# The base product of three of four token groups written as seven block products, with its weight sums in a scratch and a quarter of the low parts on GpSimd

## Chip, cores and metric

The kernel runs on one core of a Trainium2 chip (trn2). The metric is the device time of one execution in microseconds. The engines are TensorE (PE; its weight loads are PEld), VectorE (DVE), ScalarE (ACT), GpSimd (POOL) and SyncE (SP), which only issues transfers here.

## What is computed

A gated block on 2 x 1024 tokens of 2048 features: first an attention-like product of quantized numbers, then a dense layer with a routed low-rank adapter.

```python
x = x + tanh(g_xattn) * matmul(fake_quant(layernorm(x)), fake_quant(ctx_4096))
h = layernorm(x)
base = einsum('bsd,od->bso', h, base_W)                   # 2048 x 2048 x 2048, float32
probs = softmax(einsum('bsd,ed->bse', h, router_W))       # 8 experts
w_dense = top-2 of probs, scaled to sum 1, else 0
mid = einsum('bsd,edr->bser', h, lora_A) * w_dense[..., None]   # rank 16
x = x + tanh(g_ffn) * (base + 2.0 * einsum('bser,erd->bsd', mid, lora_B))
```

## The kernel before

**First stage (0 to about 305 us).** The 16 token tiles of 128 rows are normalised and quantized, `ctx` is quantized to bf16 (ScalarE, then `ctx_widen` on GpSimd), and TensorE computes 64 units (a token tile by 512 columns, 16 matmuls each) in the order of a table, `UNITS`. VectorE takes each unit out of PSUM (`evac`), and GpSimd adds a column term (`add_col_term`). When all tiles of a token group have a block, ScalarE's queue stores it to a scratch in HBM, `x1s` (`store_x1`). Tables of slots (`UNIT_SLOT`, `COLADD_SLOT` and others) set the order in which each engine takes its work; every engine walks the same slots and works in the order in which it finds its own. Its time is set by waits on semaphores, not by the slot number.

**Second stage.** Four groups `g` of 512 tokens (`M` = 4 tiles) follow. Rows of a group come back from `x1s` (`load_group`), VectorE takes their statistics and normalises them, TensorE transposes them (`transpose_h`), and ScalarE and VectorE split each transposed slice in two float32r parts, `hT_hi` and `hT_lo` (`h_hi`, `h_lo`). The weights come in pieces of 128x1024 (`WK` = 2 slices of the 2048 inputs by `NW` = 512 outputs) through a ring of four: ScalarE copies the high part (`w_hi`), VectorE subtracts to get the low part (`w_lo`). A float32 product is three matmuls (`three`): high by high, high by low, low by high. A group runs over `NB` = 4 blocks of 512 outputs; a piece feeds 2 slices x 4 tiles x 3 = 24 matmuls. At the end of a block the adapter's product (three matmuls a tile) is added in the same bank, VectorE adds the residual (L823), and the rows are stored. Behind a group the next one's router and adapter input are computed (`ar_slice`, 128 matmuls of 272 columns). Groups 0 to 2 are a loop on every engine (`Fori`), the last is written out.

## Time and profile before

| | |
|---|---|
| Times of 3 runs | 1162.58, 1166.63 (median), 1169.81 us |
| Profiled execution | 1168.86 us, of which span 1167.1 us |
| Mean granted clock of TensorE | 0.982 of full speed |
| Busy: TensorE, its weight loads, VectorE, ScalarE, GpSimd | 94%, 70%, 47%, 26%, 16% |
| Moved by DMA | 195.98 MB, 168 GB/s over the span |

The span runs from the first instruction to the last. The shares are means over both stages; GpSimd works in the first one only.

### The profile page before, as it was taken

How to read it: one execution, taken by the hardware profiler on the slowest of the kernel's cores; microseconds unless marked ns; L12 is line 12 of the kernel's file. 1: busy time of each engine (PE TensorE's matmuls, PEld its weight loads, DVE VectorE, ACT ScalarE, POOL GpSimd, SP SyncE). 2: the span in 40 equal slices, each digit the busy share in tenths (PEclk: the TensorE clock that was granted, in tenths of full speed). 3: DMA queues.
4: the chain of work that ended last, by engine and by line, in shares of the span. 5: the costliest groups of instructions: out<-in, count | busy, mean ns of one | idle time of the engine just before them, and what ended most of it. 6: DMA issues, size and time to landing. Idle time of an engine off the chain costs nothing.

```text
span 1167.1 us, 13452 instructions
## 1 busy us (share of the span) xinstructions
PE 1092.7 (94%) x5136; PEld 817.9 (70%) x5136; DVE 547.9 (47%) x832; ACT 301.5 (26%) x299; POOL 185.8 (16%) x123
## 2 busy tenths in 40 slices
PE   0679996999899999998999999989999999999998
PEld 0234442444698888887888887878888889888887
DVE  7696567955763542443238234333633343222231
ACT  5554244600232212221212213211212331111210
POOL 3584768743200000000000000000000000000000
PEclk9999998999899999998999999989999999999999
DMA  8897797757662533507242623441533504152440
GB/s 332 297 340 238 278 292 252 240 144 255 217 251 75 199 95 140 183 34 289 72 143 74 217 88 128 136 194 58 191 115 102 198 34 147 54 203 83 147 145 37
DMA packets 90699, 195.98 MB, mean 168 GB/s; under 512 B 38928, under 2 KB 40976, under 8 KB 82448
## 3 DMA queue, kind: packets, MB, share of 16 engines
q1 hardware_dynamic: 39696, 153.18, 35.6%
q10 hardware_dynamic: 50944, 41.95, 12.6%
q8 instruction: 45, 0.74, 0.3%
q14 instruction: 14, 0.11, 0.0%
HBM read 153.16 MB, written 33.55 MB: 160 GB/s over the span
## 4 chain that ended last, share of the span: by engine, by line
PE 84%; issue 3%; DVE 3%; ACT 3%; DMA 2%; POOL 2%; ACTq 2%; SPq 0%; DVEq 0%; POOLq 0%
PE acc L877 18%; PE acc L879 18%; PE acc L878 18%; PE acc L855 14%; PE acc_even L877 3%; PE acc_even L878 3%; PE acc_even L879 3%; ACTq L503 2%; PE aT_psum L892 1%; PE aT_psum L914 1%; PE aT_psum L915 1%; ACT ctx_u L490 1%; POOL ctx_quant L435 1%; DMA w_stage<-in_wt 1%; PE acc L914 1%
## 5 line engine op out<-in xcount | busy, mean ns | idle before, releaser
L877 PE MATMUL acc<-w_hi,hT_hi 128*128 128x512 f32 x896 | 354.2, 395 | 0.0
L879 PE MATMUL acc<-w_hi,hT_lo 128*128 128x512 f32 x896 | 350.6, 391 | 0.0
L878 PE MATMUL acc<-w_lo,hT_hi 128*128 128x512 f32 x896 | 350.3, 391 | 0.0
L732 DVE TENSOR_TENSOR w_lo<-w_stage,w_hi 128x1024 fp32r<-128x1024 f32 x128 | 156.7, 1224 | 320.8 <-ACT w_hi L544 319.3
L544 ACT ACTIVATE w_hi<-w_stage 128x1024 fp32r<-128x1024 f32 x128 | 135.6, 1059 | 460.1 <-PE acc L879 324.3
L879 PEld LDWEIGHTS acc<-w_hi,hT_lo 128*128 128x128 f32 x896 | 169.0, 189 | 36.2
L878 PEld LDWEIGHTS acc<-w_lo,hT_hi 128*128 128x128 f32 x896 | 169.3, 189 | 34.0
L877 PEld LDWEIGHTS acc<-w_hi,hT_hi 128*128 128x128 f32 x896 | 169.2, 189 | 34.0
L855 PE MATMUL acc<-ctx_quant,aT_even 128*128 128x512 bf16 x512 | 117.0, 388 | 43.5 <-POOL ctx_quant L435 41.1
L855 PEld LDWEIGHTS acc<-ctx_quant,aT_even 128*128 128x128 bf16 x512 | 50.4, 100 | 108.7 <-issue 44.7
L855 PE MATMUL acc<-ctx_quant,aT_odd 128*128 128x512 bf16 x512 | 115.6, 388 | 7.8 <-POOL ctx_quant L435 5.8
L855 PEld LDWEIGHTS acc<-ctx_quant,aT_odd 128*128 128x128 bf16 x512 | 50.8, 100 | 71.7 <-issue 14.2
L490 ACT ACTIVATE ctx_u<-ctx_stage,scalars,constants 128x2048 uint8<-128x2048 f32 x32 | 66.4, 2087 | 72.5 <-issue 50.5
L823 DVE SCALAR_TENSOR_TENSOR residual<-acc,gates,residual 128x512 f32<-128x512 f32 x56 | 42.0, 750 | 69.7 <-PE acc L879 69.7
L435 POOL TENSOR_SCALAR ctx_quant<-ctx_u 128x2048 bf16<-128x2048 uint8 x32 | 64.3, 2011 | 51.0 <-ACT ctx_u L490 44.7
L743 DVE TENSOR_TENSOR hT_lo<-aT_psum,hT_hi 128x512 fp32r<-128x512 f32 x48 | 32.6, 690 | 67.6 <-ACT hT_hi L552 67.6
L877 PE MATMUL acc_even<-w_hi,hT_hi 128*128 128x512 f32 x128 | 51.2, 400 | 7.7 <-issue 7.7
L552 ACT ACTIVATE hT_hi<-aT_psum 128x512 fp32r<-128x512 f32 x48 | 28.0, 597 | 96.5 <-PE aT_psum L892 96.5
L878 PE MATMUL acc_even<-w_lo,hT_hi 128*128 128x512 f32 x128 | 50.4, 394 | 0.0
L879 PE MATMUL acc_even<-w_hi,hT_lo 128*128 128x512 f32 x128 | 50.3, 393 | 0.0
L449 POOL TENSOR_TENSOR x_group_odd<-x_group_odd,col_term 128x512 f32<-128x512 f32 x32 | 43.3, 1358 | 36.0 <-DVE x_group_odd L671 36.0
L449 POOL TENSOR_TENSOR x_group_even<-x_group_even,col_term 128x512 f32<-128x512 f32 x32 | 42.2, 1333 | 20.8 <-DVE x_group_even L671 10.7
(126 smaller groups left out, 977.0 us busy)
## 6 DMA issues: line engine op xcount, KB each, us to landing
w_stage<-in_wt SPq DMA_DIRECT2D x128, 512.0 KB, 5.9
ctx_stage<-in_ctx SPq DMA_DIRECT2D x32, 1024.0 KB, 7.7
x_group_even<-x_scratch SPq DMA_DIRECT2D x16, 1024.0 KB, 10.0
residual<-x_scratch SPq DMA_DIRECT2D x64, 256.0 KB, 3.9
out<-residual ACTq DMA_DIRECT2D x64, 256.0 KB, 2.8
x_group_even<-in_x SPq DMA_DIRECT2D x8, 1024.0 KB, 7.1
x_group_odd<-in_x SPq DMA_DIRECT2D x8, 1024.0 KB, 9.7
x_scratch<-x_group_even ACTq DMA_DIRECT2D x8, 1024.0 KB, 5.6
```

What stands on the lines that cost most here:

```text
L435: pool.tensor_scalar(ctxq[:, c % NB, PK * p:PK * (p + 1), :], cu8[q % 2][:, :, :], -MID, 1.0, ALU.add, ALU.mult).then_inc(c_conv, 1)
L449: pool.tensor_tensor(blk, blk, colb[n][:, :], ALU.add).then_inc(x1_ready, 1)
L490: act.activation(cu8[q % 2][:, :, :], cst[q % CS][:, :, :], ACT.Identity, scale=inv2, bias=z2).then_inc(cu8_ready, 1)
L544: act.activation(wh[s][:, :], wst[s][:, :], ACT.Copy).then_inc(wh_ready, 1)
L552: act.activation(hh[:, k, :], h_psum(g, k), ACT.Copy).then_inc(hh_ready, 1)
L732: dve.tensor_tensor(wl[s][:, :], wst[s][:, :], wh[s][:, :].bitcast(F32), ALU.subtract)\
L743: dve.tensor_tensor(hl[:, k, :], h_psum(g, k), hh[:, k, :].bitcast(F32), ALU.subtract)\
L823: dve.scalar_tensor_tensor(out=res[m][:, :], in0=bank(j, m)[:, :], scalar=gate2, in1=res[m][:, :], op0=ALU.mult, op1=ALU.add)\
L855: ins = pe.matmul(acc[p % M][:, :], aT[g % 2][:, k, m * P:(m + 1) * P], ctxq[:, c % NB, k, :], start=(k == 0), stop=(k == K - 1))
L877: pe.matmul(out_, lh, rh, start=first, stop=False)
L878: pe.matmul(out_, lh, rl, start=False, stop=False)
L879: return pe.matmul(out_, ll, rh, start=False, stop=final)
```

## The change

Group 0 keeps its product. In groups 1 to 3 the 512 x 2048 x 2048 product is cut in two halves of outputs, and each half (512 tokens x 2048 inputs x 1024 outputs) in two by two blocks of each operand: A11, A12, A21, A22 of the tokens, transposed (256 tokens by 1024 inputs each), and B11 to B22 of the weights. It is then computed as seven block products instead of eight, in Winograd's form of Strassen's algorithm. With S1 = A21 + A22, S2 = S1 - A11, S3 = A11 - A21, S4 = A12 - S2 and T1 = B12 - B11, T2 = B22 - T1, T3 = B22 - B12, T4 = T2 - B21 (up to signs) the products are those of `COMBO` with `RIGHT`. One product is a *slot*: two token tiles x 8 slices x 3 = 48 matmuls, fed by four pieces of which each serves 12 matmuls. A group has 14 slots; `ROLE` and `FRESH` say in which pair of PSUM banks a slot works and whether it adds to what stands there. Seven times in each half of a group VectorE adds a pair of banks to one of three accumulators (`add_out`), and four of the seven are then stored.

- The weight sums T1 to T4 are computed once, by GpSimd, in eight jobs (`t_job`, four instructions of 128x1024 each), and stored to a scratch in HBM, `w_sums_scratch`. Three jobs stand in the first stage (`JOB_A_SLOT`), five in group 0.
- The token sums S1 to S4 are computed by GpSimd (`combo`) and one difference by VectorE (`diff`), ScalarE and VectorE split all of them in high and low parts (`combo_round`, `combo_rest`). For the next group this stands in slots 11 to 14 and in slot 1.
- All pieces (also the router's, which are loaded again in each group, and the adapter's) go through one list, `PIECES`: a ring of six for the loaded and the low part (`RAW`), a ring of four for the high part (`HI`). High and low parts are made three pieces ahead, loads are asked for five ahead. In groups 1 to 3 GpSimd makes the low part of one piece of each slot (`on_pool`).
- A group's normalised rows are transposed earlier, during slots 5, 6, 7 and 10 (`fill`). Nothing is a loop any more; all groups are written out.

```diff
--- before.py
+++ after.py
-WG = NB * WP
-RING = 4
-LEAD = 2 * RING
-CHAIN_B = 58
+RAW = 6
+HI = 4
...
+SLOTS_G = 14
+JOBS = 8
+JOBS_A = 3
+JOB_A_SLOT = [2120, 2260, 2400]
+RAW_B = ("B11", "B21", "B12", "B22")
+SUM_B = ("T1", "T4", "T3", "T2")
+COMBO = ("A11", "S1", "S2", "S4", "S3", "A12", "A22")
+RIGHT = ("B11", "T1", "T2", "B22", "T3", "B21", "T4")
+ROLE = (0, 1, 0, 1, 0, 1, 0)
+FRESH = (True, True, False, False, False, True, False)
+LORA = (None, None, None, "top_right", "bottom_right", "top_left", "bottom_diff")
+CBUF = (0, 2, 1, 1, 2, 0, 1)
+LOADS_RES = (True, True, True, False, False, False, True)
+STORES = (False, False, False, True, True, True, True)
...
+def on_pool(i):
+    g, kind, s, pc = PIECES[i]
+    return g >= 1 and kind == "W" and pc == 1
...
+    half, r = (s - 1) // 7, (s - 1) % 7
+    return 2 * ((ROLE[r] + half) % 2) + part
...
+            def load_piece(i):
+                g, kind, s, pc = PIECES[i]
+                raw = wst[i % RAW]
+                if i >= RAW:
+                    wait_used(sp, i - RAW)
+            def store_job(j):
+                sp.wait_ge(job_step, 4 * (j + 1))
+                dst = wts[(j // 4) * 2 * WP * P:(j // 4 + 1) * 2 * WP * P, :]
+                sp.dma_start(dst.rearrange("(a q p) n -> q p a n", q=4, p=P)[j % 4], job[j][:, :, :])\
+                    .then_inc(job_stored[j], 16)
...
+            load_job(0)
+            load_job(1)
+            store_job(0)
+            load_job(2)
             sp.wait_ge(x1_stored[0], 16 * NB * 2)
-            load_group(0)
-            sp.wait_ge(pe_unit, max(last_of_tile(t) for t in range(2 * M, 3 * M)) + 1)
-            for r in range(RING):
-                load_lead(r, r)
-            for X in range(RING):
-                sp.wait_ge(wl_ready, X + 1)
-                load_w(X)
+            load_group0()
+            store_job(1)
+            sp.wait_ge(c_conv, 2 * NB * CP)
+            sp.wait_ge(job_stored[1], 16)
+            for i in range(RAW - 1):
+                load_piece(i)
+            store_job(2)
...
+            def t_job(j):
+                pool.wait_ge(job_in[j], 16)
+                b11, b21, b12, b22 = (job[j][:, a, :] for a in range(4))
+                pool.tensor_tensor(b11, b12, b11, ALU.subtract).then_inc(job_step, 1)
+                pool.wait_ge(job_step, 4 * j + 1)
+                pool.tensor_tensor(b12, b22, b12, ALU.subtract).then_inc(job_step, 1)
+                pool.wait_ge(job_step, 4 * j + 2)
+                pool.tensor_tensor(b22, b22, b11, ALU.subtract).then_inc(job_step, 1)
+                pool.wait_ge(job_step, 4 * j + 3)
+                pool.tensor_tensor(b21, b21, b22, ALU.subtract).then_inc(job_step, 1)
             for s in range(SLOTS):
+                if s in JOB_A_SLOT:
+                    t_job(JOB_A_SLOT.index(s))
...
+            def w_lo(i):
+                pool.wait_ge(wh_ready, i + 1)
+                pool.tensor_tensor(wl[i % RAW][:, :], wst[i % RAW][:, :], wh[i % HI][:, :].bitcast(F32),
+                                   ALU.subtract).then_inc(wl_by_pool, 1)
+
+            def combo(dst, a, b, op, h):
+                pool.tensor_tensor(half(dst, h), half(a, h), half(b, h), op).then_inc(combo_sum, 1)
+
+            for i, (g, kind, s, pc) in enumerate(PIECES):
+                if i + HI - 1 < N_PIECES and on_pool(i + HI - 1):
+                    w_lo(i + HI - 1)
...
+                    if s == 12 and pc in (0, 1):
+                        pool.wait_ge(s3_diff, 2 * g + pc + 1)
+                        if pc == 0:
+                            pool.wait_ge(acc_done, done_count(g, 10, 1))
+                        combo(csum["S2"], hf["A22"], hf["A11"], ALU.subtract, pc)
+                    if s == 12 and pc in (2, 3):
+                        if pc == 2:
+                            pool.wait_ge(acc_done, done_count(g, 11, 1))
+                        combo(csum["S4"], hf["A12"], hf["A22"], ALU.subtract, pc - 2)
+                    if s == 13 and pc in (0, 1):
+                        pool.wait_ge(combo_sum, sum_count(g, "S4", pc))
+                        combo(csum["S4"], csum["S4"], hf["A11"], ALU.add, pc)
...
+            def w_hi(i):
+                g, kind, s, pc = PIECES[i]
+                act.wait_ge(w_in[i % RAW], 16 * (i // RAW + 1))
+                if i >= HI:
+                    wait_used(act, i - HI)
...
+                if ends_slot(i - 1):
+                    add_out(*PIECES[i - 1][0:3:2])
+                ahead = i + HI - 1
+                if ahead < N_PIECES:
+                    if not on_pool(ahead):
+                        w_lo(ahead)
...
+                    if s == 11 and pc in (1, 2):
+                        combo_rest(g, "A11", pc - 1)
+                    if s == 11 and pc == 3:
+                        for h in range(2):
+                            diff(g, h)
+                    if s == 12 and pc in (2, 3):
+                        combo_rest(g, "S1", pc - 2)
+                    if s == 13 and pc in (1, 2):
+                        combo_rest(g, "S2", pc - 1)
+                    if s == 13 and pc == 3 or s == 14 and pc == 0:
+                        combo_rest(g, "S3", pc == 0)
+                    if s == 14 and pc in (1, 2):
+                        combo_rest(g, "S4", pc - 1)
+                    if s == 14 and pc == 3:
+                        for h in range(2):
+                            combo_rest(g, "A12", h)
...
+            def slot(g, s):
+                r = (s - 1) % 7
+                name = COMBO[r]
+                high, low = chi[name], clo[name]
+                pe.wait_ge(combo_lo, refill_count(g - 1, name, 1))
+                for pc in range(4):
+                    i = INDEX[g, "W", s, pc]
+                    wait_lo(pe, i)
+
+                    def product(t, kk):
+                        k, part = WK * pc + kk, slice(kk * NW, (kk + 1) * NW)
                         if k == 0:
-                            pe.wait_ge(out_ready, g * ITS + ITS)
-
-            with pe.Fori(0, G - 1) as g:
-                group(g, False)
-            group(G - 1, True)
+                            pe.wait_ge(c_added, bank_free(g, s, t))
+                        last = LORA[r] is None and k == HK - 1
+                        return three(bank(g, s, t)[:, :], high[:, k, tok(t)], low[:, k, tok(t)], wh[i % HI][:, part],
+                                     wl[i % RAW][:, part], FRESH[r] and k == 0, last, not FRESH[r])
...
+            for g in range(1, G):
+                for s in range(1, SLOTS_G + 1):
+                    slot(g, s)
+                    if s == 1:
+                        for k in range(K):
+                            ar_slice(g, k)
```

**The order on GpSimd, end of the first stage.** Before (rows `x_group_...<-..., col_term` are `add_col_term`):

```order
99 L449 TENSOR_TENSOR x_group_even<-x_group_even,col_term_64 128x512
100 L449 TENSOR_TENSOR x_group_odd<-x_group_odd,col_term_65 128x512
101 L449 TENSOR_TENSOR x_group_even<-x_group_even,col_term_67 128x512 x2
102 L449 TENSOR_TENSOR x_group_odd<-x_group_odd,col_term_64 128x512
103 L449 TENSOR_TENSOR x_group_odd<-x_group_odd,col_term_65 128x512 x2
104 L449 TENSOR_TENSOR x_group_odd<-x_group_odd,col_term_66 128x512
105 L449 TENSOR_TENSOR x_group_odd<-x_group_odd,col_term_67 128x512
106 L449 TENSOR_TENSOR x_group_odd<-x_group_odd,col_term_66 128x512 x2
```

and now:

```order
103 L682 TENSOR_TENSOR x_group_even<-x_group_even,col_term_64 128x512
104 L682 TENSOR_TENSOR x_group_odd<-x_group_odd,col_term_65 128x512
105 L682 TENSOR_TENSOR x_group_even<-x_group_even,col_term_67 128x512
106 L687 TENSOR_TENSOR t_job_128<-t_job_128 128x1024
107 L689 TENSOR_TENSOR t_job_128<-t_job_128 128x1024
108 L691 TENSOR_TENSOR t_job_128<-t_job_128 128x1024
109 L693 TENSOR_TENSOR t_job_128<-t_job_128 128x1024
110 L682 TENSOR_TENSOR x_group_even<-x_group_even,col_term_67 128x512
111 L682 TENSOR_TENSOR x_group_odd<-x_group_odd,col_term_64 128x512
112 L682 TENSOR_TENSOR x_group_odd<-x_group_odd,col_term_65 128x512 x2
113 L687 TENSOR_TENSOR t_job_129<-t_job_129 128x1024
114 L689 TENSOR_TENSOR t_job_129<-t_job_129 128x1024
```

Weight-sum jobs stand between the adds: here job 1 (`t_job_128`) ahead of the last add for group 2's tiles, and then job 2.

**The order on VectorE, end of a group.** Before, in the last block of a loop turn (`hT_lo` is the next group's low part, read from PSUM):

```order
458 L823 SCALAR_TENSOR_TENSOR residual_87<-acc,gates,residual_87 128x512
459 L821 REGISTER_ALU
460 L823 SCALAR_TENSOR_TENSOR residual_88<-acc,gates,residual_88 128x512
461 L731 REGISTER_ALU
462 L732 TENSOR_TENSOR w_lo_79<-w_stage_71,w_hi_75 128x1024
463 L742 REGISTER_ALU
464 L743 TENSOR_TENSOR hT_lo<-aT_psum,hT_hi 128x512
465 L742 REGISTER_ALU
466 L743 TENSOR_TENSOR hT_lo<-aT_psum,hT_hi 128x512
467 L731 REGISTER_ALU
468 L732 TENSOR_TENSOR w_lo_76<-w_stage_68,w_hi_72 128x1024
```

and now, slots 11 and 12 of group 1 (`c_acc` rows are `add_out`, `A_lo` and `S_lo` are `combo_rest`, `hT_A_88` is `diff`):

```order
519 L1219 SCALAR_TENSOR_TENSOR c_acc_99<-acc,gates,c_acc_99 128x512 x2
520 L1145 TENSOR_TENSOR w_lo_119<-w_stage_113,w_hi_105 128x1024
521 L1143 TENSOR_TENSOR w_lo_120<-w_stage_114,w_hi_102 128x512
522 L1246 TENSOR_TENSOR A_lo<-hT_A_88,A_hi 128x1024
523 L1145 TENSOR_TENSOR w_lo_121<-w_stage_115,w_hi_103 128x1024
524 L1246 TENSOR_TENSOR A_lo<-hT_A_88,A_hi 128x1024
525 L1237 TENSOR_TENSOR hT_A_88<-hT_A_88,hT_A_90 128x1024 x2
526 L1219 SCALAR_TENSOR_TENSOR c_acc_99<-acc,gates,c_acc_99 128x512 x2
527 L1145 TENSOR_TENSOR w_lo_117<-w_stage_111,w_hi_105 128x1024
528 L1145 TENSOR_TENSOR w_lo_118<-w_stage_112,w_hi_102 128x1024
529 L1143 TENSOR_TENSOR w_lo_119<-w_stage_113,w_hi_103 128x512
530 L1145 TENSOR_TENSOR w_lo_120<-w_stage_114,w_hi_104 128x1024
```

The halves of combinations, of which each reads two tensors in SBUF, stand between the low parts of the pieces.

**The order on GpSimd, the same place.** Before, its queue ended with the first stage's last add. Now, slots 11 to 14 of group 1 (`S_sum` rows are `combo`):

```order
159 L707 TENSOR_TENSOR w_lo_117<-w_stage_111,w_hi_103 128x1024
160 L711 TENSOR_TENSOR S_sum<-hT_A_90,hT_A_91 128x1024 x2
161 L707 TENSOR_TENSOR w_lo_116<-w_stage_110,w_hi_104 128x1024
162 L711 TENSOR_TENSOR S_sum<-hT_A_91,hT_A_88 128x1024 x2
163 L711 TENSOR_TENSOR S_sum<-hT_A_89,hT_A_91 128x1024
164 L707 TENSOR_TENSOR w_lo_121<-w_stage_115,w_hi_105 128x1024
165 L711 TENSOR_TENSOR S_sum<-hT_A_89,hT_A_91 128x1024
166 L711 TENSOR_TENSOR S_sum<-S_sum,hT_A_88 128x1024 x2
167 L707 TENSOR_TENSOR w_lo_120<-w_stage_114,w_hi_102 128x1024
168 L707 TENSOR_TENSOR w_lo_119<-w_stage_113,w_hi_103 128x1024 x2
```

Two, three or one of the sums stand between two low parts that TensorE waits for.

## Rows read from the trace of the kernel before

**Rows 1.** The page: the span, and each engine's busy time (share) and instructions.
```profile
span 1167.1 us, 13452 instructions
...
PE 1092.7 (94%) x5136; PEld 817.9 (70%) x5136; DVE 547.9 (47%) x832; ACT 301.5 (26%) x299; POOL 185.8 (16%) x123
```

**Rows 2.** TensorE's timeline: start, length (us), engine, line, operation, shapes; idle before.
```profile
401.01 0.39 PE L877 MATMUL acc<-w_hi,hT_hi 128*128 128x512 f32 x1
401.24 0.39 PE L878 MATMUL acc<-w_lo,hT_hi 128*128 128x512 f32 x1
...
542.91 0.28 PE L914 MATMUL aT_psum<-ar_hi_lo,hT_hi 128*128 128x272 f32 x1
543.03 0.29 PE L915 MATMUL aT_psum<-ar_hi_lo,hT_lo 128*128 128x272 f32 x1
547.16 0.79 PE L877 MATMUL acc_even<-w_hi,hT_hi 128*128 128x512 f32 x1 [3.84 <-issue]
...
552.34 0.40 PE L877 MATMUL acc_even<-w_hi,hT_hi 128*128 128x512 f32 x1
```

**Rows 3.** Who TensorE waits for, 302 us on: us in total, times, longest.
```profile
PE acc_even L877 <- issue: 7.7, 2, 3.8
PE acc L914 <- DVE ar_hi_lo L724: 2.4, 1, 2.4
```

**Rows 4.** Windows: length; busy PE, PEld, DVE, ACT, POOL; granted clock, DMA share, GB/s.
```profile
543.30:547.00 3.70, 0.02 (x1) 0.00 (x0) 3.36 (x16) 0.23 (x1) 0.00 (x0) 0.78 1.01 421
547.00:551.00 4.00, 3.84 (x9) 3.08 (x10) 3.42 (x15) 0.00 (x0) 0.00 (x0) 0.50 1.00 410
```

**Rows 5.** Groups by line and shape from 333 us on: busy us, mean ns of one.
```profile
L732 DVE TENSOR_TENSOR w_lo<-w_stage,w_hi 128x1024 fp32r<-128x1024 f32 x124 | 151.8, 1224 | 319.8 <-ACT w_hi L544 318.3
...
L823 DVE SCALAR_TENSOR_TENSOR residual<-acc,gates,residual 128x512 f32<-128x512 f32 x56 | 42.0, 750 | 69.7 <-PE acc L879 69.7
...
L738 DVE TENSOR_TENSOR b_lo<-w_stage,b_hi 128x512 fp32r<-128x512 f32 x2 | 1.3, 684 | 0.0
...
L544 ACT ACTIVATE w_hi<-w_stage 128x1024 fp32r<-128x1024 f32 x124 | 131.4, 1060 | 460.1 <-PE acc L879 324.3 <-DMA w_stage<-in_wt 135.8
```

**Rows 6.** GpSimd's timeline in the first stage.
```profile
27.88 1.97 POOL L441 TENSOR_SCALAR x_group_even<-x_group_even,row_terms 128x2048 f32<-128x2048 f32 x1 [0.79 <-DVE row_terms L648]
...
37.32 1.90 POOL L435 TENSOR_SCALAR ctx_quant<-ctx_u 128x2048 bf16<-128x2048 uint8 x1 [2.07 <-ACT ctx_u L490]
39.20 4.00 POOL L441 TENSOR_SCALAR x_group_even<-x_group_even,row_terms 128x2048 f32<-128x2048 f32 x1
...
262.77 1.27 POOL L449 TENSOR_TENSOR x_group_even<-x_group_even,col_term 128x512 f32<-128x512 f32 x1 [2.19 <-DVE x_group_even L671]
```

**Rows 7.** VectorE's timeline beside it.
```profile
37.81 3.55 DVE L656 TENSOR_TENSOR ctx_pair_sums<-ctx_quant 128x4096 f16<-128x4096 bf16 x1
...
108.50 2.28 DVE L656 TENSOR_TENSOR ctx_pair_sums<-ctx_quant 128x4096 f16<-128x4096 bf16 x1
```

**Rows 8.** The end of the first stage on all engines, from their timelines.
```profile
244.47 1.98 POOL L441 TENSOR_SCALAR x_group_odd<-x_group_odd,row_terms 128x2048 f32<-128x2048 f32 x1 [7.17 <-DVE row_terms L648]
...
253.71 10.74 ACTq L510 DMA_DIRECT2D x_scratch<-x_group_even  x2
...
268.25 2.06 SPq L350 DMA_DIRECT2D x_group_even<-x_scratch  x4
...
279.81 2.46 DVE L608 BATCH_NORM_STATS2 bn_chunks_group<-x_group_even 128x6 f32<-128x512 f32 x4
...
305.44 0.66 PE L892 MATMUL acc_even<-identity_f,x_group_even 128*128 128x128 f32 x4 [2.15 <-DVE x_group_even L686]
...
309.70 0.57 PE L914 MATMUL acc<-ar_hi_lo,hT_hi 128*128 128x272 f32 x1 [2.35 <-DVE ar_hi_lo L724]
```

**Rows 9.** DMA issues: how often, KB each, median us from issue to landing.
```profile
w_stage<-in_wt SPq DMA_DIRECT2D x128, 512.0 KB, 5.9
...
x_group_even<-x_scratch SPq DMA_DIRECT2D x16, 1024.0 KB, 10.0
```

More of the change, by code:

```diff
@@ new lines, with pieces @@
+LOADS_RES = (True, True, True, False, False, False, True)
+STORES = (False, False, False, True, True, True, True)
+REFILL = {0: ("S1", "S2", "S3", "A11", "S4", "A21", "A12", "A22"),
+          1: ("A11", "S1", "S2", "S3", "S4", "A12", "A21", "A22")}
+def pieces():
+    order = [(0, "AR", 0, pc) for pc in range(WP)]
+    for n in range(NB):
+        order += [(0, "W", n + 1, pc) for pc in range(WP)] + [(0, "L", n + 1, WP)]
+    for g in range(1, G):
+        for s in range(1, SLOTS_G + 1):
+            order += [(g, "W", s, pc) for pc in range(4)]
+            if LORA[(s - 1) % 7]:
+                order.append((g, "L", s, 4))
+            if s == 1:
+                order += [(g, "AR", 1, pc) for pc in range(WP)]
+    return order
@@ new lines, with lo_count, ends_slot, done_count @@
+PIECES = pieces()
+INDEX = {piece: i for i, piece in enumerate(PIECES)}
+N_PIECES = len(PIECES)
+def on_pool(i):
+    g, kind, s, pc = PIECES[i]
+    return g >= 1 and kind == "W" and pc == 1
+def lo_count(i, pool):
+    return sum(on_pool(e) == pool for e in range(i + 1))
+def ends_slot(i):
+    if i < 0:
+        return False
+    g, kind, s, pc = PIECES[i]
+    return kind == "W" and pc == (WP - 1 if g == 0 else 3)
+def done_count(g, s, part):
+    return M * (s - 1) + part + 1 if g == 0 else M * NB + 2 * SLOTS_G * (g - 1) + 2 * (s - 1) + part + 1
@@ new lines, in closes, with used_count, bank_of, bank_free @@
+def closes(i):
+    g, kind, s, pc = PIECES[i]
+    if kind == "AR":
+        return "ar" if pc == WP - 1 else None
+    if kind == "L" or ends_slot(i) and g >= 1 and not LORA[(s - 1) % 7]:
+        return "slot"
+    return None
+def used_count(i):
+    return sum(closes(e) is None for e in range(i + 1))
+def bank_of(g, s, part):
+    if g == 0:
+        return "even" if part == 0 and s % 2 == 1 else part
+    half, r = (s - 1) // 7, (s - 1) % 7
+    return 2 * ((ROLE[r] + half) % 2) + part
+def bank_free(g, s, part):
+    history = [(0, n + 1, m) for n in range(NB) for m in range(M)]
+    history += [(a, b, t) for a in range(1, G) for b in range(1, SLOTS_G + 1) for t in range(2)]
+    mine = history.index((g, s, part))
+    before = [h for h in history[:mine] if bank_of(*h) == bank_of(g, s, part)]
+    return done_count(*before[-1]) if before else 0
@@ L137, in __call__, with build @@
             self.eng.wait_ge(self.sem, self.base + self.n)
-def build(nc, x, ctx, wt, ar, lb, scal, x1s, out):
+def build(nc, x, ctx, wt, ar, lb, scal, x1s, wts, out):
     es = ExitStack()
@@ L236, in build, with bank @@
         acc0b = psum("acc0_even", [P, NW], F32)
-        def bank(j, m):
-            return acc0b if m == 0 and j % 2 == 0 else acc[m]
-        arp = [acc[0], colp, tpb[0], tpb[1]]
+        def bank(g, s, part):
+            b = bank_of(g, s, part)
+            return acc0b if b == "even" else acc[b]
+        arp = [[acc[0] if g == 0 else acc0b, colp, tpb[0], tpb[1]] for g in range(G)]
         th0 = [acc0b, acc[1], acc[2]]
@@ L415, in _ @@
+            uses = (NB + 2 * (G - 1), NB + 4 * (G - 1), 2 * (G - 1))
+            for b in range(3):
+                sp.wait_ge(out_stored[b], 32 * uses[b])
         @block.gpsimd
@@ L980, in _, with plain_product @@
-            with pe.Fori(0, G - 1) as g:
-                group(g, False)
-            group(G - 1, True)
+                    transpose_h(k + 3)
+            def plain_product(n, pp, m, kk):
+                i = INDEX[0, "W", n + 1, pp]
+                k, part = WK * pp + kk, slice(kk * NW, (kk + 1) * NW)
+                if k == 0:
+                    if bank_free(0, n + 1, m):
+                        pe.wait_ge(c_added, bank_free(0, n + 1, m))
+                    if n == 1 and m == 0:
+                        pe.wait_ge(mid_read, 1)
+                high, low = h_parts(0, k, m)
+                return three(bank(0, n + 1, m)[:, :], high, low, wh[i % HI][:, part], wl[i % RAW][:, part],
+                             k == 0, False)
```

956 lines of the change are left out of this document (664 added, 292 removed).

## The prediction

> **What bounds the kernel now.** The page comes first: TensorE is busy for 94% of the 1167.1 us span, VectorE for 47%, ScalarE for 26%, and GpSimd has done all of its 16% before the first 305 us are over [rows 1]. The busy time of a pipelined TensorE doesn't say that it runs at its pace, so the second view is its own timeline. In the base product a 128x512 matmul starts 0.227 us after the one before (401.01, 401.24), and a router matmul of 272 columns 0.125 us after [rows 2]. The base stage is therefore TensorE's row of matmuls, one behind another: VectorE and ScalarE wait for it, not it for them. The view of waits bears that out: from 302 us on its longest total is 7.7 us, at the two returns of the group loop, where nothing in the profile releases it, and the next is 2.4 us, once, on the way into group 0 [rows 3]. At 543 us TensorE stands for 3.84 us, and the 12 matmuls behind it take 547.16 to 552.34, 5.18 us, where 12 x 0.227 = 2.72 is the pace; the granted clock is 0.50 there, the lower level, 1.2 GHz [rows 2, 4]. Each return thus costs 3.7 + 2.5 = 6.2 us.
>
> **What is removed.** A group had 4 blocks x 16 slices x 4 token tiles x 3 = 768 base matmuls. In groups 1 to 3 it becomes 14 slots x 8 slices x 2 tiles x 3 = 672. The adapter's 48 and the router's 128 stay, and so do the 64 transposes of a group. So 3 x 96 = 288 matmuls go, at 0.227 us each: 65.3 us, all of it on the path. The group loops are written out, so both returns go as well: 2 x 6.2 = 12.4 us. Bounds of that: nothing (a fetch wait stays somewhere) and 12.4; the straight code of the last group has no such wait [rows 3], so I take 12.4. TensorE alone would give 1167.1 - 65.3 - 12.4 = 1089.4 us. The tail is of the same kind as before (one addition, one store).
>
> **What the shorter product asks of the other engines.** A piece of weights (128x1024) used to feed 24 matmuls, 5.44 us; now it feeds 12, 2.72 us, and 56 pieces are prepared in a group, not 32. ScalarE's high part takes 1.06 us and VectorE's low part 1.22 [rows 5], both shorter than 2.72. High and low parts are made three pieces ahead: 8.2 us less 1.1 + 1.2 for the work leaves some 5.8 us by which VectorE may be late before TensorE stands. The part of an adapter piece is wanted already when the slot's last piece begins, so there it is 3 us. On average all fits; what counts is where the new work is bunched.
>
> **The end of a group is such a place.** Slots 11 to 14 hold 4 x 54 = 216 matmuls, 49.0 us. In them VectorE (second fence of the change's order) makes 12 low parts and 14 halves of combinations at 1.22 us, four adapter parts and a difference at 0.68, and 8 additions at 0.75: 31.8 + 3.4 + 6.0 = 41.2 us. GpSimd makes 4 low parts and 8 sums, each 128x1024 with two inputs in SBUF. Its add of 128x512 takes 1.26 to 1.27 us [rows 6], so twice that, 2.5 us: 12 x 2.5 = 30 us. Side by side, both fit into 49.
>
> Do they run side by side? The rows say no. VectorE's pair sum, two inputs in SBUF, takes 2.28 us alone (108.50), but 3.55 at 37.81: GpSimd's instruction of 37.32 ends at 39.2, and 39.2 + 2.3 is its end. GpSimd's row term, 1.97 us alone, takes 4.00 at 39.20, since VectorE's sum runs until 41.4 [rows 6, 7]. Each stood until the other was through. If float32 instructions do the same, VectorE's 35.2 us with two SBUF inputs and GpSimd's 30 have to follow one another: 65 us in 49. The 16 us too many, less the lead of 5.8, leave about 10.5 us that TensorE waits; VectorE's additions read PSUM and don't exclude GpSimd, but hold up its next low part, and an adapter part has the shorter lead. I take 12 us a transition, two of them (from 1 to 2 and from 2 to 3; the last group has no sums): 24 us. Bounds: 0, if the lock doesn't hold here or the next 27 us (slot 1 and the router) take up the rest, and 20 each if additions and waits for each other's results add up. The nearest rows are the two at 37 and 39 us, so I stay near the middle.
>
> The Trainium skill has a rule for it (SBUF — State Buffer, Who interferes with whom): a VectorE instruction with two SBUF inputs contends with a GpSimd instruction that reads SBUF, whoever is first holds the shared pair for its whole length, and the other blocks. It speaks against giving low parts to GpSimd. By that rule the 24 us stand; by each engine's own durations alone they would be 0, and the sum 1105. The trace agrees with the rule at 37.81 and 39.20, for bf16 and for one-input GpSimd work; no row of it has two float32 tensor_tensor beside each other.
>
> **The way into group 1** has the old and the new form together. In the first three pieces of slot 1 VectorE has 4 additions and 8 halves of combinations (S4, A21, A12, A22) besides its low parts, about 12.2 us in two pieces of 2.72, and ScalarE 8 copies at 1.06. The router's third slice pair then comes about 3.5 us late and its first waits about 1: 5 us, bounds 0 and 10. In each of the three groups the adapter's low part stands behind a tile's statistics on VectorE while slot 4's last piece waits for it: 1 us each, 3 in all, bounds 0 and 9.
>
> **The end of the first stage.** GpSimd gets three weight-sum jobs of four 128x1024 instructions, 10 us each, ahead of adds that it made at once. Job 0 can start at 246.4, after the row term of 244.47 [rows 8]. It ends at 256.6, seven adds catch up until 265.4, job 1 ends at 275.5, and the last add of group 2's tiles comes at 276.8; its store was issued at 264 (253.71 + 10.74), and is now near 277. Before, the loads of group 0's rows were issued at 268.25, 4 us behind; now at 281. Their median landing was 10.0 us for four in a row [rows 9]; I put the first at 287, an estimate. So VectorE's statistics start there and not at 279.81 [rows 8]. Since VectorE is nearly always busy from there until TensorE's first transpose at 305.44, that moves by about the same 7 to 8 us; TensorE's units themselves have four banks and go on. The next thing late is the adapter and router weights, whose ring lies where job 2's data were: its store is queued behind four megabytes and ends near 311 (an estimate from 421 GB/s). So the first router slice, at 309.70 before, comes near 318: **+8 us**, bounds 1 (the loads had time to spare) and 18 (jobs also late by their own loads).
>
> **Transfers.** A group of 187 us moves 29 MB of weights, 5 of adapter and router weights, 4 of rows and 8 of residuals and output: 46 MB, 246 GB/s. At 543 us the queues moved 421 GB/s [rows 4], so the rate is there. A piece is asked for five pieces ahead, 13.6 us; less 2.3 for its parts it must land in 11. It took 5.9 us, 10.0 where four loads of a megabyte stood in a row [rows 9]. I take 0. In group 0 the jobs add 20 MB to about 20 over 115 us, 350 GB/s, with a lead of 27 us: 0 too.
>
> **The sum.** 1089.4 + 8 + 5 + 24 + 3 = 1129.4 us of span. The profiled execution has 1.8 us around its span and lies 2.2 us above the median of the three runs (1168.86, 1166.63), so 1131.2 as profiled and **1129** as the median.
>
> **Rivals.**
> - *All hidden.* The lock costs nothing that the lead doesn't cover, since GpSimd's sums are wanted only slots later. Then 1089.4 + 4 + 2 + 2, about 1098 (1088 to 1110). For it: over a whole group VectorE and GpSimd together need less than TensorE. Against: 65 us in 49 at the end of a group.
> - *The lock costs double.* If each low part stands behind one of GpSimd's sums every time, and the lower clock follows the stops as at 547 us, a transition costs 20 to 25 and other slots a few: 1145 to 1165.
> - *The weight ring starves, slower than before.* Its place is the load of a piece in groups 1 to 3. If it lands L us after issue, a piece can't go faster than (L + 2.3) / 5. From L = 11.3 TensorE waits at every piece. With the 8 us of the first stage alone, 1167 is passed when each of the 168 pieces takes 0.42 us more, 3.14, which is L = 13.4. At L = 15 it is 3.46 a piece, 124 us in all, near 1220. For it: 10.0 in [rows 9], where requests queue, and each megabyte of rows goes in front of pieces. Against: the rate shown.
> - *The product is not shorter in effect.* If accumulating over an old result in PSUM made matmuls slower than 0.227, 10% would eat the gain. Every matmul but a bank's first accumulates today at this pace; small.
>
> **How the numbers follow.** 40% for the forecast's own case (1112 to 1145), 28% all hidden, 15% the double price, 10% starved or another stop of every slot (above 1178), 7% something between 1155 and 1178. The range leaves out about 15 to 20%: 1094 to 1160. A measurement can tell about 1% here, 1155 to 1178 being no change: faster 0.82 (the first two and most of the third), same 0.08, slower 0.10.
>
> **What would show it.** Matmul spacing 0.227 us in the slots, and no stop of 3.84 us. GpSimd rows of 2.5 us that lengthen to 3.7 and VectorE rows of 1.22 that lengthen up to 3.7, most of all in slots 11 to 14; there TensorE waits for a low part of VectorE's, 8 to 15 us a transition. The first router slice near 318. Were TensorE's waits to name the DMA of a weight piece, the third rival holds; were there none at all in slots 11 to 14, the first. What would make me wrong above all is the size of the queue at the group's end, which was worked out from a lead and two sums.

## The result, and the profile after

| | before | after |
|---|---|---|
| Median (lowest to highest) | 1166.74 us (1162.58 to 1169.81, 4 runs) | 1133.87 us (1127.80 to 1137.54, 4 runs) |
| Ratio, 95% interval | | 0.9715 [0.9662, 0.9768] |
| Profiled execution: span | 1167.1 us | 1125.8 us |

The profiled execution took 1127.8 us, the fastest of its four; a second series of the same kernel (below) had a median of 1131.27 us. The forecast was 1129, with a span of 1129.4.

The page of the changed kernel, first its busy times (answers to [rows 1]), then the landing of DMAs ([rows 9]):

```profile
span 1125.8 us, 12711 instructions
...
PE 1031.9 (92%) x4827; PEld 765.3 (68%) x4848; DVE 745.4 (66%) x1004; ACT 448.2 (40%) x480; POOL 449.3 (40%) x223
...
w_stage<-in_wt SPq DMA_DIRECT2D x104, 512.0 KB, 4.4
w_stage<-w_sums_scratch SPq DMA_DIRECT2D x96, 512.0 KB, 4.2
```

TensorE has 309 matmul records fewer (288 went; some are missing from a trace). GpSimd's share went from 16% to 40%, and it is no longer done at 305 us. Weight pieces land sooner after they are asked for than before, 4.4 us against 5.9 in the median; some are asked for late (E9, below).

Who TensorE waits for from 300 us on (total, times, longest), the view that answers to [rows 3]:

```profile
PE acc_even L1393 <- DVE x_group_even L1099: 8.1, 1, 8.1
PE acc L1381 <- DVE w_lo L1145: 7.9, 7, 3.4
PE acc L1381 <- DVE w_lo L1143: 6.3, 2, 3.2
PE aT_psum L1451 <- DVE x_rows L1231: 4.7, 3, 3.1
PE acc L1429 <- DVE ar_hi_lo L1140: 3.1, 1, 3.1
PE acc L1381 <- DVE c_acc L1219: 2.3, 1, 2.3
```

The two stops of 3.8 us that nothing released are gone. In their place are stops in which VectorE is late: at the end of the first stage (8.1 and 3.1), for low parts (14.2 in nine waits, of which 11.6 lie in the two transitions and the rest in slot 4), and in group 0 for a normalised row and an addition (`x_rows`, 3.1 of the 4.7, and `c_acc`). No wait of TensorE names the DMA of a weight piece.

The first transition, TensorE's timeline: the wait for the adapter piece's low part, then one piece at the product's pace, then the next stop and what follows it.

```profile
707.80 0.47 PE L1381 MATMUL acc<-w_hi,S_hi 128*128 128x512 f32 x1 [3.17 <-DVE w_lo L1143]
...
709.95 0.39 PE L1381 MATMUL acc<-w_hi,S_hi 128*128 128x512 f32 x1
710.18 0.39 PE L1382 MATMUL acc<-w_lo,S_hi 128*128 128x512 f32 x1
...
721.02 0.80 PE L1381 MATMUL acc<-w_hi,A_hi 128*128 128x512 f32 x1 [3.42 <-DVE w_lo L1145]
...
724.17 0.63 PE L1382 MATMUL acc<-w_lo,A_hi 128*128 128x512 f32 x1
724.60 0.63 PE L1383 MATMUL acc<-w_hi,A_lo 128*128 128x512 f32 x1
```

The spacing is 0.227 us with accumulation over an old result, as in [rows 2]; behind the second stop it is 0.43 until 726.3, and the window of that stretch (busy times as in [rows 4], then granted clock) shows the lower level, 1.2 GHz:

```profile
721.00:726.00 5.00, 4.98 (x12) 3.92 (x13) 5.00 (x5) 1.36 (x2) 0.00 (x0) 0.50 0.29 112
```

VectorE and GpSimd in the same stretch, from their timelines:

```profile
688.04 3.42 DVE L1246 TENSOR_TENSOR A_lo<-hT_A,A_hi 128x1024 fp32r<-128x1024 f32 x1
691.38 1.21 DVE L1145 TENSOR_TENSOR w_lo<-w_stage,w_hi 128x1024 fp32r<-128x1024 f32 x1
...
699.45 5.45 DVE L1145 TENSOR_TENSOR w_lo<-w_stage,w_hi 128x1024 fp32r<-128x1024 f32 x2
704.82 2.83 DVE L1143 TENSOR_TENSOR w_lo<-w_stage,w_hi 128x512 fp32r<-128x512 f32 x1
707.57 3.42 DVE L1145 TENSOR_TENSOR w_lo<-w_stage,w_hi 128x1024 fp32r<-128x1024 f32 x1
```

```profile
684.60 5.78 POOL L711 TENSOR_TENSOR S_sum<-hT_A,hT_A 128x1024 f32<-128x1024 f32 x2 [4.49 <-ACT hT_A L877]
...
697.15 9.95 POOL L711 TENSOR_TENSOR S_sum<-hT_A,hT_A 128x1024 f32<-128x1024 f32 x3 [1.16 <-DVE hT_A L1237]
707.07 2.84 POOL L707 TENSOR_TENSOR w_lo<-w_stage,w_hi 128x1024 fp32r<-128x1024 f32 x1
709.87 3.39 POOL L711 TENSOR_TENSOR S_sum<-hT_A,hT_A 128x1024 f32<-128x1024 f32 x1
```

The low part of 1.21 us at 691.38 runs while GpSimd stands. Beside GpSimd's sums the same instruction takes 2.7, an `A_lo` that begins beside one takes 3.42, which is one of GpSimd's (2.2) and its own (1.2); and GpSimd's take 3.3 instead of 2.4. Both engines read as busy all the time, and a good part of that time is the other's work.

The end of the first stage, GpSimd's jobs among its adds, the store's waiting loads, VectorE's statistics and TensorE ([rows 8] before):

```profile
264.63 2.35 POOL L687 TENSOR_TENSOR t_job<-t_job 128x1024 f32<-128x1024 f32 x1
...
274.22 1.27 POOL L682 TENSOR_TENSOR x_group_even<-x_group_even,col_term 128x512 f32<-128x512 f32 x1
...
279.68 3.26 SPq L518 DMA_DIRECT2D x_group_even<-x_scratch  x4
...
286.88 2.47 DVE L1021 BATCH_NORM_STATS2 bn_chunks_group<-x_group_even 128x6 f32<-128x512 f32 x4 [7.71 <-DMA x_group_even<-x_scratch]
...
310.63 1.12 PE L1393 MATMUL acc_even<-identity_f,x_group_even 128*128 128x128 f32 x4 [8.08 <-DVE x_group_even L1099]
316.54 0.36 PE L1429 MATMUL acc<-ar_hi_lo,hT_hi 128*128 128x272 f32 x1 [3.08 <-DVE ar_hi_lo L1140]
```

And a place that the prediction did not have, in group 0: VectorE beside a weight-sum job, first VectorE, then GpSimd.

```profile
454.93 0.15 DVE L1026 RECIPROCAL rstd<-std 128x1 f32<-128x1 f32 x1
...
455.56 2.06 DVE L1033 TENSOR_TENSOR rstd<-rstd,newton 128x1 f32<-128x1 f32 x1
457.66 3.45 DVE L1231 TENSOR_SCALAR x_rows<-x_rows,mean_var,rstd 128x2048 f32<-128x2048 f32 x1
```

```profile
455.18 2.43 POOL L687 TENSOR_TENSOR t_job<-t_job 128x1024 f32<-128x1024 f32 x1 [19.51 <-DMA t_job<-in_wt]
457.68 2.34 POOL L689 TENSOR_TENSOR t_job<-t_job 128x1024 f32<-128x1024 f32 x1
460.10 3.21 POOL L691 TENSOR_TENSOR t_job<-t_job 128x1024 f32<-128x1024 f32 x1
```

`rstd<-rstd,newton` has one element a partition and takes 0.16 us elsewhere; here it ends when GpSimd's instruction does (457.62 and 457.61). The row normalisation behind it takes 3.45 us instead of 1.35, and TensorE stands 3.12 us for it at 461.16.

**Where the span went**, against the 1089.4 us that TensorE alone would take:

| place | expected | measured |
|---|---|---|
| end of the first stage (first router slice 309.70, now 316.54) | 8 | 6.8 |
| group 0: waits at 390 and 461, 5.4, and 1.3 of lower clock | 0 | 6.7 |
| way into group 1 | 5 | 0.9 |
| adapter's low part behind the statistics, slot 4 (601, 801, 1000 us) | 3 | 2.8 |
| two transitions: waits 7.2 and 4.5, lower clock 2.7 in each | 24 | 9.9 + 7.2 |
| small waits elsewhere (0.47, 0.24, 1.38) | 0 | 2.1 |
| sum with 1089.4 | 1129.4 | 1125.8 |

That the right column ends at the span exactly is partly luck: E1 puts what the loop returns cost at 2.4 us more than the 12.4 that lead to 1089.4, and about as much is lost in pieces of 0.1 to 0.4 us, mostly behind the stops, which the table doesn't list. The 1.38 is a wait for `x_rows` at 873.97, in group 2; E9 shows what is behind it.

### The profile page after: what moved, and what is told of

Read it like the earlier page. It is cut to its first block, busy times and chain, and to the rows that moved or that the text cites. A ratio compares the mean times of both kernels' runs of the same rounds, so it can differ in the third digit from the quotient of the medians.

```text
span 1125.8 us, 12711 instructions
## 1 busy us (share of the span) xinstructions
PE 1031.9 (92%) x4827; PEld 765.3 (68%) x4848; DVE 745.4 (66%) x1004; ACT 448.2 (40%) x480; POOL 449.3 (40%) x223
## 3 DMA queue, kind: packets, MB, share of 16 engines
q10 hardware_dynamic: 50944, 41.95, 12.8%
## 4 chain that ended last, share of the span: by engine, by line
PE 63%; DVE 14%; DMA 7%; issue 6%; ACT 4%; POOL 4%; ACTq 2%; SPq 1%; another core or an unknown queue 0%; POOLq 0%; DVEq 0%
PE acc L1381 15%; PE acc L1383 14%; PE acc L1382 14%; PE acc L1359 10%; DVE w_lo L1145 4%; DMA w_sums_scratch<-t_job 3%; PE aT_psum L1451 2%; DMA w_stage<-w_sums_scratch 2%; DVE S_lo L1246 2%; ACTq L809 1%; PE aT_psum L1429 1%; PE aT_psum L1430 1%; ACT ctx_u L796 1%; DVE A_lo L1246 1%; POOL ctx_quant L668 1%
## 5 line engine op out<-in xcount | busy, mean ns | idle before, releaser
L707 POOL TENSOR_TENSOR w_lo<-w_stage,w_hi 128x1024 fp32r<-128x1024 f32 x42 | 104.8, 2496 | 405.9 <-ACT w_hi L854 405.9
L1381 PE MATMUL acc<-w_hi,S_hi 128*128 128x512 f32 x384 | 152.8, 398 | 10.3 <-DVE w_lo L1143 6.3
L1383 PE MATMUL acc<-w_hi,S_lo 128*128 128x512 f32 x384 | 150.5, 392 | 0.0
L1382 PE MATMUL acc<-w_lo,S_hi 128*128 128x512 f32 x384 | 150.3, 391 | 0.0
L1381 PE MATMUL acc<-w_hi,A_hi 128*128 128x512 f32 x288 | 115.4, 401 | 4.4 <-DVE w_lo L1145 4.4
L1383 PE MATMUL acc<-w_hi,A_lo 128*128 128x512 f32 x288 | 113.3, 393 | 0.0
L1382 PE MATMUL acc<-w_lo,A_hi 128*128 128x512 f32 x288 | 113.2, 393 | 0.0
L1381 PE MATMUL acc<-w_hi,hT_hi 128*128 128x512 f32 x224 | 87.9, 392 | 2.3 <-DVE c_acc L1219 2.3
L1383 PE MATMUL acc<-w_hi,hT_lo 128*128 128x512 f32 x224 | 87.3, 390 | 0.0
L1382 PE MATMUL acc<-w_lo,hT_hi 128*128 128x512 f32 x224 | 87.2, 389 | 0.0
```

Of the source, the lines that this page charges most:

```text
L707: pool.tensor_tensor(wl[i % RAW][:, :], wst[i % RAW][:, :], wh[i % HI][:, :].bitcast(F32), ALU.subtract).then_inc(wl_by_pool, 1)
L1381: pe.matmul(out_, lh, rh, start=first, stop=False, skip_group_check=onto)
L1382: pe.matmul(out_, lh, rl, start=False, stop=False, skip_group_check=onto)
L1383: return pe.matmul(out_, ll, rh, start=False, stop=final, skip_group_check=onto)
```

## The experiments

All were timed against the kernel before on the same chip; ratios are to it. A second series of the changed kernel itself, beside E5 to E7:

> The changed kernel itself, for the comparison on the same chip: ratio 0.970 to 0.973 to the kernel before, span 1124 to 1128, and the same waits of TensorE (14 us for low parts in the two transitions, 5.4 us at 390 and 461).

1131.27 us (6 runs), 0.9707 [0.9676, 0.9737]. Its profiled execution was a long one (span 1131.8); the waits for low parts are 12.7 us there (10.1 in the two transitions; the 14 expected for these counted slot 4 in), and 12.4 for `x_rows`, `c_acc` and `hT_A` in group 0 and the rows of group 2. Most places are the same, their sizes vary by some us. At 466.78 TensorE waits 5.2 us for `x_rows` where it was 3.1: here two of VectorE's small instructions met one of GpSimd's job (2.16 and 2.20 us), in the first profile one (2.06).

**E1: the loops alone, before.**

```diff
-            with pe.Fori(0, G - 1) as g:
+            for g in range(G - 1):
```
(on all four engines)

> The kernel before, with its group loop written out on all four engines and nothing else changed. Theory: the two stops of 3.84 us at the loop's returns and the slow matmuls behind them go, 12 us, ratio to before about 0.989. Rival: the stop is a wait for instructions that straight code has too, somewhere else, so the time stays within 3 us of before. In the changed kernel no such stop is seen, so I expect the first.

1153.16 us, 0.9893 [0.9871, 0.9914]. Its waits from 302 us on:

```profile
PE acc L914 <- DVE ar_hi_lo L724: 2.4, 1, 2.4
PE acc_even L892 <- DVE x_group_even L686: 2.2, 1, 2.2
```

Both waits are there before the change too. The stops without a releaser are gone and nothing took their place: 11.5 us on the same chip's medians (10.0 to 15.0 by the interval). In the traces, from one group's first router matmul to the next group's, the two loop turns took 217.5 and 217.2 us, and take 210.0 each here: 14.8 us, with all that followed the stops. By the medians that is a seventh of the 77.7 us that the change saves before its losses, and has nothing to do with the product.

**E2: all low parts on VectorE.**

```diff
 def on_pool(i):
-    return g >= 1 and kind == "W" and pc == 1
+    return False
```

> The changed kernel with all low parts on VectorE; GpSimd keeps its sums. Lock theory: a low part holds the shared access to SBUF for 1.2 us on VectorE and 2.4 on GpSimd, so in slots 11 to 14 the two together need 60 us instead of 65, and TensorE waits less at the end of groups 1 and 2: 0 to 5 us a transition, 0 to 8 us in all faster than the changed kernel. Rival, each engine's own load: VectorE needs 46 us of the 49 instead of 41 and its low parts come later by 4 x 1.2 us, so TensorE waits 3 to 5 us more in each transition, 5 to 15 us slower.

1127.23 us, 0.9666 [0.9641, 0.9691], no slower than the changed kernel, and its waits for low parts are 9.8 us instead of 14.2 (8.3 for 11.6 in the transitions):

```profile
PE acc L1381 <- DVE w_lo L1143: 5.9, 2, 3.0
...
PE acc L1381 <- DVE w_lo L1145: 3.9, 4, 1.6
```

Giving GpSimd a quarter of the low parts relieves VectorE of nothing.

**E3: the jobs of the first stage later.**

```diff
-JOB_A_SLOT = [2120, 2260, 2400]
+JOB_A_SLOT = [2120, 2352, 2440]
```

> The changed kernel with the second and third weight-sum job later in GpSimd's order of the first stage (slots 2352 and 2440 for 2260 and 2400), so that the last add of group 2's tiles stands ahead of job 1. Theory of the prediction: the rows of group 0 are loaded some 10 us earlier, VectorE's statistics start near 280 again, TensorE's first transpose comes near 305 for 310.6. The first router slice then waits for job 2's store, which ends about where it did or 3 us later, so of the 6.8 us at most 4 are won: first router slice at 313 to 318. Rival: the statistics wait for something else (the loads' own traffic), and the first transpose stays at 310.

1130.12 us, 0.9703 [0.9671, 0.9735]. The statistics begin at 279.97, 7 us earlier, and the first router slice at 311.55, 5 us earlier, so the job ahead of group 2's last add was the cause. But the waits for `x_rows` are 5.5 us in group 0 and 2.2 in group 2 in this run (3.1 and 1.4 before), and those for low parts 15.7, so the span, 1126.8, shows none of it: a gain at one place was within the variation at others.

**E4: the adapter's low part ahead of the statistics.**

```diff
-                    if s == 4 and pc == 2:
+                    if s == 4 and pc == 1:
                         mid_lo(g)
```
(placed before `row_stats`)

> The changed kernel with the low part of the transposed adapter input ahead of the row statistics in VectorE's order of slot 4 (one piece earlier). TensorE's waits of 1.6, 0.9 and 0.4 us at the last piece of slot 4 (601, 801, 1000 us) go, 2.8 us in all, 0.25%, under what timing can tell; the rows at those three places tell it. Rival: the piece's low part then comes late by itself and the wait stays.

1128.74 us, 0.9694 [0.9662, 0.9726]. The three waits at slot 4 are gone; the span, 1126.9, is no shorter, with 7.7 us for `x_rows` (5.2 of them in group 0).

**E5: all low parts and the token sums of groups 1 to 3 on VectorE.** `combo` in slots 11 to 13 moves, in the same order, from GpSimd's queue to VectorE's.

```diff
-                        combo(csum["S1"], hf["A21"], hf["A22"], ALU.add, pc - 1)
+                        dve_sum(csum["S1"], hf["A21"], hf["A22"], ALU.add, pc - 1)
```

> In groups 1 to 3 all low parts and all token sums S1, S2, S4 stand on VectorE; GpSimd does nothing there but its weight-sum jobs of the first stage and of group 0. Theory A (VectorE and GpSimd shut each other out of SBUF, so that the two rows of work follow one another at the end of a group): without GpSimd VectorE has 41.2 + 12 x 1.22 = 56 us of work in the 49 us of slots 11 to 14, all at its own short durations (1.22 us a row, none above 1.5), and TensorE's waits for low parts in the two transitions fall from 14 us to 1 to 7; span 1114 to 1124. Theory B (each engine's load alone decides, no lock): taking 30 us of work from GpSimd and giving it to VectorE makes VectorE's queue 15 us longer, and TensorE's waits there grow by 8 to 15 us a transition: span 1140 to 1155.

1114.50 us, 0.9578 [0.9554, 0.9601]; span 1106.1. No wait of TensorE names a low part any more; of slot 4's waits 1.4 us are left, for which the view names no releaser. VectorE at the same place:

```profile
697.82 2.35 DVE L1127 TENSOR_TENSOR w_lo<-w_stage,w_hi 128x1024 fp32r<-128x1024 f32 x2
700.09 1.22 DVE L1223 TENSOR_TENSOR S_sum<-hT_A,hT_A 128x1024 f32<-128x1024 f32 x1
701.22 0.69 DVE L1125 TENSOR_TENSOR w_lo<-w_stage,w_hi 128x512 fp32r<-128x512 f32 x1
701.82 1.22 DVE L1223 TENSOR_TENSOR S_sum<-hT_A,hT_A 128x1024 f32<-128x1024 f32 x1
```

Every instruction has its short duration, and a sum takes VectorE 1.22 us where GpSimd needs 2.4. With 15 us more work at the end of a group VectorE is not late: of the two theories only the lock allows that. The move also does away with VectorE's and GpSimd's waits for each other's results, but those are idle time between instructions and can't be what made the instructions themselves long. Even the 1 to 7 us that were expected to stay in the transitions are not there.

**E6: GpSimd's jobs without their work.**

```diff
-                b11, b21, b12, b22 = (job[j][:, a, :] for a in range(4))
+                b11, b21, b12, b22 = (job[j][:, a, 0:8] for a in range(4))
```

The instructions work on 8 of 1024 columns, so this kernel leaves most of the weight sums out and does not compute the block; its time alone is of use.

> Leaves out nearly all of the arithmetic of the weight sums (each of the 32 instructions of the eight jobs works on 8 columns of 1024); their loads, stores and order stay, so the weights of four of seven products are mostly the unchanged ones. Theory A (GpSimd's jobs are what delays the end of the first stage and what holds VectorE's row normalisation in group 0): the statistics of group 0 start near 280 instead of 287, the first router slice comes near 310 instead of 316.5, and the waits of 2.3 us near 390 and 3.1 us near 461 are gone: 10 to 13 us less than the changed kernel, span 1113 to 1116. Rival B (those waits come from the later place of the loads behind the job's store and from DMA traffic, not from GpSimd's instructions): statistics stay near 285 to 287 and the waits in group 0 stay, less than 3 us gained.

1118.01 us, 0.9616 [0.9599, 0.9634]; span 1112.0. Statistics at 278.63, first router slice at 309.67, where it was before the change (309.70), and no wait near 390 or 461. Between the jobs' loads and stores, which are still there, and their instructions, it is the instructions that cost: 13.8 us of span. TensorE still waits 3.9 us for the router's weights at 309.67, as in E10.

**E7: E2, E3 and E4 together**, and in group 0 the last row normalised one piece earlier.

> All low parts on VectorE, the second and third weight-sum job of the first stage behind the adds of group 2's tiles, the adapter input's low part ahead of the tile statistics, and the last row of a group normalised one piece earlier in group 0. If the three gains seen one by one add (4.4 us of waits for low parts, 5 us in the first stage, 2.8 us at slot 4) and the row normalisation has room: span 1113 to 1119, median 1116 to 1122. If they are given back at group 0's row normalisation, which stands behind GpSimd's jobs all the same: span 1123 to 1127, no better than the changed kernel.

1114.01 us, 0.9567 [0.9551, 0.9582]; span 1109.6, better than the sum that was expected. `x_rows` costs 1.1 us, none of it in group 0, low parts still 9.5. What E3 and E4 gained and lost again, most of it in group 0, is kept here.

**E9: E7 with the token sums of groups 1 to 3 on VectorE. E10: the five jobs and the sums of group 0 on VectorE too.**

```diff
+                    if 1 <= at_piece <= 20:
+                        dve_job((at_piece - 1) // 4 + JOBS_A, (at_piece - 1) % 4)
```

> The combined kernel with the token sums of groups 1 to 3 on VectorE too, so that GpSimd is silent from group 1 on. Theory A (SBUF lock between VectorE and GpSimd): the 9.5 us of waits for low parts in the two transitions and the lower clock behind them go, as they went when the sums alone were moved: span 1094 to 1099, median 1097 to 1103. Theory B (VectorE's load alone): no gain on the combined kernel, 1108 or more.

> As the one before, and the five weight-sum jobs and the token sums of group 0 on VectorE as well, one job instruction a piece: GpSimd is silent behind the first stage. Theory A: the waits near 387 (2.3 us for an addition) and for the normalised rows in group 0 go, a further 2 to 4 us: span 1091 to 1096. Rival: VectorE's 30 more instructions of 1.22 us (37 us in 218) meet the row normalisation and the additions in the same way as GpSimd's lock did, and the waits stay: span as the one before, within 1 us, or longer.

E9: 1101.09 us, 0.9447 [0.9427, 0.9467]. Its profiled execution was its longest, 1110.09 us, and its rows show waits at two kinds of places. In group 0, where GpSimd still works, TensorE waits 4.0 us for `c_acc` and 3.5 for `hT_A`. And in groups 1 and 2, where GpSimd is silent, it waits 2.9 and 1.3 us for `x_rows`. The chain of the first of these, from SyncE's wait (view of 655 to 666 us) to TensorE:

```profile
SPq L571 <- DMA out<-c_acc: 7.3, 1, 7.3
...
664.73 1.42 SPq L537 DMA_DIRECT2D w_stage<-w_sums_scratch  x3
...
670.11 1.06 ACT L836 ACTIVATE w_hi<-w_stage 128x1024 fp32r<-128x1024 f32 x1 [4.09 <-DMA w_stage<-w_sums_scratch]
...
674.45 1.35 DVE L1213 TENSOR_SCALAR x_rows<-x_rows,mean_var,rstd 128x2048 f32<-128x2048 f32 x1
...
675.85 0.66 PE L1453 MATMUL aT_psum<-identity_f,x_rows 128*128 128x128 f32 x4 [2.89 <-DVE x_rows L1213]
```

A load of residuals stands ahead of the weight pieces in SyncE's order and waits until an output is stored, so the pieces behind it are asked for late; VectorE, which works in order, has the row's normalisation behind the low part of such a piece. This has nothing to do with GpSimd. The same chain is behind the 1.4 us at 873.97 in the changed kernel (SyncE waited 4.7 us there) and behind the waits for `x_rows` of 2.6 us at 679.90 in its second series and 2.2 in group 2 of E3. This is read from the traces; no run changed that order.

E10: **1095.88 us, 0.9404 [0.9381, 0.9427]**, span 1094.1. All that TensorE waits for in E10 from 300 us on, but for three of 0.5 and less:

```profile
PE acc L1440 <- DVE ar_hi_lo L1097: 4.8, 1, 4.8
PE acc_even L1404 <- DVE x_group_even L1056: 3.8, 1, 3.8
PE aT_psum L1462 <- ACT hT_A L834: 1.7, 1, 1.7
PE acc_even L1440 <- DVE ar_hi_lo L1097: 0.9, 1, 0.9
```

VectorE makes 200 low parts with a mean of 1222 ns, as in [rows 5], and TensorE's clock is 1.00 in every window from 336 us on. The 1.7 us for `hT_A` have stayed with GpSimd silent, so that wait is not the lock's alone. The 4.8 us end with a store: ScalarE's high part of the router's first weights lies where job 2's data were, and waits until these are stored.

```profile
311.00 0.43 ACT L804 ACTIVATE ar_hi_lo<-w_stage 128x272 fp32r<-128x272 f32 x1 [15.25 <-DMA w_sums_scratch<-t_job]
```

E10 and E1, both without loop and without a wait inside a full group, give the price of the product itself: from the first router matmul of group 2 to that of group 3 the time is 188.0 us in E10 and 210.0 in E1. That is 22.0 us less for 96 matmuls fewer, which at 0.227 us are 21.8. The sum 1089.4 + 3.7 (first router slice at 313.38) + 0.9 (way into group 1) = 1094.0 comes within 0.1 us of E10's span, but it leaves out the 1.7 us for `hT_A` and two waits of 0.5 and 0.3 in group 0, which stand against the 2.4 us that the loop returns cost beyond 12.4.

## Why the prediction was right

**Right, with its mechanism.** 288 matmuls at 0.227 us, 21.8 a group: the spacing is in the rows, and E10 against E1 gives 22.0 a group. Two loop returns: 12.4 forecast, 11.5 in E1's medians and 14.8 in the traces. VectorE and GpSimd shutting each other out of SBUF: forecast as 2.5 to 3.7 and 1.22 to 3.7 us a row, measured 2.4 to 3.4 and 1.2 to 3.4, and E5 shows it as the cause of the transitions, since more work on VectorE alone ended them. By the Trainium skill (SBUF — State Buffer, Who interferes with whom) whoever is first holds the shared pair for its whole length and the other blocks; here the trace agrees, for two float32 instructions of 128x1024 too. The statistics were expected at 287 and began at 286.88, behind the job that was named, and E3 and E6 bear the chain out. Slot 4's 3 us were 2.8, and E4 removed them.

**Terms mis-sized.** The transitions: "I take 12 us a transition", measured 9.9 and 7.2; of that the waits for low parts are 7.2 and 4.5, where 8 to 15 were to be seen. The 65 us in 49 were summed over slots 11 to 14 as if the work were spread over them. GpSimd's last sum ends at 719.9, in slot 13; VectorE, busy without a gap from 688 on, has gaps again from 727 (1.5, 1.3, 1.1 us), and in slot 14 TensorE waits for nothing. The lateness was made in three slots, and not every row of VectorE met one of GpSimd's. The way into group 1: 5, measured 0.9, although the work listed for VectorE there, 4 additions and 8 halves, comes to 12.8 us and not to 12.2. ScalarE's and VectorE's bunch there delays the router's third slice pair by less than a microsecond, the router's 16 slices were reserve enough. The first stage: 8, measured 6.8. The statistics started where they were expected; the first transpose moved by 5.2 us (305.44 to 310.63) instead of 7 to 8, and what ended last was the store of job 2, which the prediction had named as the next thing late: ScalarE's high part of the router's weights could start at 314.16, the first slice at 316.54 and not at 318.

**A step that failed.** For group 0 the prediction took "a lead of 27 us: 0 too", and looked there only at transfers. It had the lock's rows before it and used them at the end of a group alone. It says that no row before has two float32 `tensor_tensor` beside each other, and it did not think of small instructions. But the first stage of the kernel before has such rows, and one of the two instructions is small (0.16 us elsewhere):

```profile
208.22 2.49 POOL L449 TENSOR_TENSOR x_group_even<-x_group_even,col_term 128x512 f32<-128x512 f32 x2
```

```profile
208.48 1.02 DVE L620 TENSOR_TENSOR x_rstd<-x_rstd,newton 128x1 f32<-128x1 f32 x1
```

The first of GpSimd's two adds ends near 209.47, and VectorE's instruction of one element at 209.50. The five jobs of group 0 are 50 us of GpSimd, and beside them VectorE's row normalisation, with a piece's time to spare, and its additions were held up: 6.7 us in the profile, more in other runs. E6 removes these waits, and E10 all but 0.3 us of them. The transfers, "I take 0", failed in a small way: the prediction looked at rates and landing times, not at SyncE's order, in which a residual load that waits for a store delays the pieces behind it (E9; 1.4 us in the profile). The errors have opposite signs: 6.7 and 2.1 us were missing, 12.4 were too much elsewhere. That they nearly cancel, and that 1129 came so near, is luck.

**Rivals.** The starving ring did not come as it was described, slower than before: a piece landed in 4.4 us in the median and no wait of TensorE names its DMA. Pieces that were asked for late did reach TensorE by way of VectorE's order, for up to 4.1 us (E9). The lock did not cost double, 20 to 25 us a transition, and accumulation over an old result ran at the old 0.227 us. "All hidden", 1088 to 1110, is not this kernel, but it is E10's: the same product on the same rings without the lock.

What stays open: what the 3.84 us at a loop's return are, beyond that they go with the loop; why the same kernel varies by 10 us between executions. The profiles show two parts of that, how many of VectorE's small instructions meet a job's in group 0 and how late the pieces behind a residual load are, and not what sets either.

## What to carry to other kernels

Work that is given to an idle GpSimd beside a busy VectorE is not free when both read SBUF: add both engines' times in every stretch where they meet, and look at every instruction that has little time to spare, the small ones too. Here VectorE did it all better alone, at 70% busy: of the 35 us between the changed kernel and E10 (1131.27, 1095.88), 17 came by E5 alone. Look at the order of a queue too: a load that waits for a store holds up every load behind it (E9). And a gain at one place (E3, E4) may not show until the next late thing is gone; judge it by its wait in the trace, and try it again together with others.
